# Four-layer convolution chain on one core: in the third layer, numerators made half a step ahead of their quotients, and a second of eighteen squares moved from GpSimd to VectorE

## The reference

```python
def _L2_conv_ref(x, A, Bc):          # DEG_P = 6, DEG_Q = 4, 3x3 windows
    xp = jnp.pad(x, ((0, 0), (0, 0), (pad, pad), (pad, pad)))
    wins = jnp.stack([xp[:, :, i:i + H, j:j + W] for i in range(K) for j in range(K)])
    pw = wins[..., None] ** jnp.arange(DEG_P, dtype=x.dtype)
    P = jnp.einsum('pbchwi,fcpi->fpbchw', pw, A)
    Q = 1.0 + jnp.abs(jnp.einsum('pbchwi,fcpi->fpbchw', pw[..., 1:1 + DEG_Q], Bc))
    out = jnp.sum(P / Q, axis=(1, 3))
    return jnp.transpose(out, (1, 0, 2, 3))
```

## Time and profile before

| | |
|---|---|
| time, median of 3 executions | 11572.25 us (11549.52 to 11573.89) |
| profiled execution: its own time | 11549.69 us |
| profiled execution: span of the trace | 11547.8 us |
| busy over the span | PE 8600.7, DVE 8534.8, ACT 6994.4, POOL 5920.0 us |
| third layer's pairs: first q block, last | 5994.0 us, 10554.8 us after the span's start |
| products of line 1360 in the whole run | 4232 to `l_r`, 528 to `l_rc` |

### The profile page before, as it was taken

How to read it: one execution, slowest core, us unless ns; L and a number is a source line. 1 busy time by engine, 2 the same in 40 slices (tenths; PEclk the granted TensorE clock), 3 DMA queues, 4 the chain that set the end, 5 groups by cost and what they waited for, 6 DMA issues and landing times. The chain is left out here.

```text
span 11547.8 us, 174635 instructions
## 1 busy us (share of the span) xinstructions
PE 8600.7 (74%) x48250; PEld 4203.0 (36%) x48250; DVE 8534.8 (74%) x10195; ACT 6994.4 (61%) x7795; POOL 5920.0 (51%) x2841
## 2 busy tenths in 40 slices
PE   0788758884888488853018888888888888885699
PEld 0566536663666366631002222222222222221233
DVE  1787668775777478754648888888888888886677
ACT  0455435553555255533438888888888888885454
POOL 0223223221333123210039999999999999995243
PEclk9899879987999689976559999999999999997899
DMA  2000000000000100011422232223322222224444
GB/s 90 1 0 0 15 23 0 0 11 26 0 0 7 30 1 0 0 38 56 148 83 59 67 65 60 59 59 66 65 61 59 59 63 65 64 59 100 122 115 99
DMA packets 254148, 548.42 MB, mean 47 GB/s; under 512 B 38656, under 2 KB 173088, under 8 KB 239552
## 3 DMA queue, kind: packets, MB, share of 16 engines
q1 hardware_dynamic: 253366, 539.26, 19.3%
HBM read 353.17 MB, written 185.94 MB: 47 GB/s over the span
## 5 line engine op out<-in xcount | busy, mean ns | idle before, releaser
L1232 POOL TENSOR_TENSOR l_a<-l_a 128x1018 f32<-128x1018 f32 x2248 | 4282.8, 1940 | 296.4 <-ACT l_a L1398 286.6
L1360 DVE TENSOR_TENSOR l_r<-l_pps,l_a 128x509 f32<-128x509 f32 x4232 | 2641.4, 679 | 641.3 <-PE l_pps L1245 641.3
L1398 ACT ACTIVATE l_a<-l_a 128x2036 f32<-128x2036 f32 x1193 | 2268.6, 1902 | 178.0 <-DVE l_a L1366 106.4
L1391 ACT ACTIVATE l_a<-l_qps 128x1018 f32<-128x1018 f32 x1725 | 1748.1, 1020 | 531.2 <-PE l_qps L1245 494.4
L1245 PE MATMUL l_qps<-l_mv,l_wst 123*128 123x509 bf16 x4246 | 1317.1, 393 | 865.8 <-DMA l_mv<-pw 577.0
L654 POOL TENSOR_TENSOR a_pr<-a_pr 128x768 f32<-128x768 f32 x384 | 898.7, 2340 | 1639.3 <-DVE a_pr L569 1624.2
L1245 PE MATMUL l_pps<-l_mv,l_wst 123*128 123x509 bf16 x4232 | 1356.6, 389 | 145.8 <-DVE l_r L1360 137.5
L454 POOL TENSOR_TENSOR a_pr<-a_qkv 128x768 f32<-128x768 f32 x128 | 386.7, 3040 | 2065.3 <-ACT a_qkv L696 2065.3
L683 ACT ACTIVATE a_g<-a_fps 128x512 f32<-128x512 f32 x1152 | 680.6, 597 | 989.8 <-PE a_fps L436 988.4
L436 PE MATMUL a_fps<-a_hbt,a_wfc 96*128 96x512 f32 x2304 | 1217.6, 664 | 70.3 <-ACT a_g L683 70.3
L407 PEld LDWEIGHTS a_cps<-a_wfp,a_g 128*128 128x128 f32 x9216 | 1120.7, 197 | 204.6 <-issue 154.8
(11 more groups left out here) (164 smaller groups left out, 11770.4 us busy)
## 6 DMA issues: line engine op xcount, KB each, us to landing
l_mv<-pw SPq DMA_DIRECT2D x1608, 79.5 KB
l_gx<-g SPq DMA_DIRECT2D x66, 1040.0 KB
planes<-l_s SPq DMA_DIRECT2D x67, 1018.0 KB, 4.6
l_sh<-planes SPq DMA_DIRECT2D x536, 127.2 KB, 6.3
pw<-pw_hi SPq DMA_DIRECT2D x165, 127.2 KB
pw<-pw_mid SPq DMA_DIRECT2D x165, 127.2 KB
pw<-pw_lo SPq DMA_DIRECT2D x165, 127.2 KB
a_tb<-g SPq DMA_DIRECT2D x16, 1031.9 KB
```

The lines of the kernel that those rows point to most:

```text
L1232: g.tensor_tensor(a, a, a, ALU.mult).then_inc(sq_p, 1)
L1360: v.tensor_tensor(to, pps[:, (2 * m + h) % P_BANKS, 0:SUB], pair_of(A, m)[:, h, :], ALU.mult).then_inc(mul_done, 1)
L1391: s_.activation(pair_of(A, s), q, ACT.Abs).then_inc(abs_a, 1)
L1398: s_.activation(a, a, ACT.Abs_reciprocal_sqrt, bias=1.0).then_inc(root_done, GROUP)
```

## The change

The numerator blocks are numbered b = 2m and 2m + 1 for pair m. Where PE made blocks 2m and 2m + 1 in step s = m + 8, it now makes blocks 2m + 1 and 2m + 2: the second block of this step's pair and the first block of the next one. And pair 14 of each eighteen joins pair 3 in the set that DVE squares, so POOL squares 16 of 18 instead of 17. Buffers, lags and every amount of matmul work stay the same.

```diff
 ABS_DVE = {1, 5, 8, 12, 15}
-SQ_DVE = {3}
+SQ_DVE = {3, 14}
...
                     last.then_inc(q_made, 1)
-                    m = s - LAG_P
-                    if m >= 0:
-                        sub, n = divmod(m, NPAIR2)
-                        for h in range(2):
-                            pe.wait_ge(mul_done, it * (2 * STEPS) + 2 * m + h - P_BANKS + 1 + 2 * A_PAIRS)
-                            product(0, sub, 2 * n + h, pps[:, (2 * m + h) % P_BANKS, 0:SUB]).then_inc(p_made, 1)
+                    for b in (2 * (s - LAG_P) + 1, 2 * (s - LAG_P) + 2):
+                        if b >= 0:
+                            sub, n = divmod(b, NBLK)
+                            pe.wait_ge(mul_done, it * (2 * STEPS) + b - P_BANKS + 1 + 2 * A_PAIRS)
+                            product(0, sub, n, pps[:, b % P_BANKS, 0:SUB]).then_inc(p_made, 1)
```

## The result

The changed kernel takes 11725.22 us in the median of 4 executions (11708.07 to 11751.85), the kernel before 11573.07 us beside it. The ratio is 1.0128 with a 95% interval of 1.0112 to 1.0144: slower by 1.3%. The direction was forecast, the size was not: 47 us were expected above the median of before, about 150 came, and 11,725 lies above the range.

A forecast was written before the change was run, and what follows sets the result against it. The ring PE -> DVE -> PE was taken to set the pace, not POOL. The order's -1.2 and the squares' +2.1 us a supertile gave +0.9, times 66 +59 us: 11,620 us forecast, range 11,465 to 11,700.

The forecast's parts named there:

- POOL is not the bound: Third layer: POOL only fills space between ACT and DVE; the rival that POOL is the bound had 11,453 us, chance 0.1.
- The five pairs that POOL was ahead: Counts by 8058.3 us: POOL's squares reach pair 1079, DVE's products 1074 pairs, so POOL is some five pairs ahead.
- The new squares: DVE's second square, two a supertile: 1.6 - 0.5 + 1.13 = 2.2, taken as +2.1 us; bounds 1.0 and 4.0.
- The 1.13: Price in us of the second-half square, right behind the output add, where POOL idles and nothing covers it.
- The 1.6: Price in us of the first-half square by the median; some 0.5 us of it falls into an existing DVE wait.
- The order: PE's new numerator order: feeds DVE one product sooner, holds PE around squares; net -1.2 us a supertile.
- the bound of -1.9: Best case for PE's numerator order, us a supertile: the walk through one supertile with nothing lost.
- bounded that at +0.2: Worst case for PE's numerator order, us a supertile: an earlier DVE only waits longer for POOL in its square.
- the forecast of +0.9: Whole third layer: -1.2 + 2.1 us a supertile, times 66 is +59 us; the slower outcome had chance 0.48.
- the gains of the walk, 0.6 and 1.4: Numerator order, us a supertile: output add after the gather 0.6 earlier; q blocks waiting for absolute values about 1.4.
- The second cost that I named: PE's last block of a step waits one product longer; q blocks and sums 0.6 us later around DVE's square.
- signs that I had named for my own outcome: DVE idle 9.7 to some 7 us, busy over 0.88; POOL about 0.88; 265 squares, mean above 1.5; longer PE waits.

The follow-up runs named there:

- the pair of runs with one reduction: DVE's square of pair 3 replaced by a one-input reduction, pair left unsquared: kernel before 11541.81 us; kernel with the new order alone 11396.65 us.
- the pair with two: DVE's squares of pairs 3 and 14 replaced by one-input reductions, pairs left unsquared: order of before 11581.65 us, changed kernel 11499.87 us.
- both squares late: Changed kernel with DVE's squares of pairs 3 and 14 moved behind the two products of their step: 11609.21 us, ratio 1.0022.
- the run with the late square: Kernel with the new order and only pair 3 squared on DVE; that square moved behind the two products of its step: 12071.4 us, ratio 1.0416.

## Why the prediction was right about the sign and wrong about the size

**POOL is not the bound: right.** Relieving it by the second square alone cost 1.3%, loading it with DVE's squares gave 1.2%. The five pairs that POOL was ahead said more than its busy share of 940. One reason why the share misleads is in the earlier trace rows too: a POOL square of 2.86 us counts as busy for 0.98 us in which DVE's holds it up. The Trainium skill's rule (Perfetto Trace Analysis, Identifying the Most-Contended Engine), by which the engine of highest occupancy is to be relieved first, would have sent one the wrong way here.

**The new squares: right in size, and in part by luck.** Forecast were 1.6 and 1.13 us from start to start, found 1.47 and 1.12 in the supertile shown. The 1.13 had a reason that held: POOL had run out of work there. The 1.6 was the median of pair 3's squares and held only because pair 14's falls near the end of a square of POOL in the changed kernel; with the order of before it takes 2.85, 2.76 from start to start. The second square alone cost 147 us, 2.2 us a supertile, where the sum had 2.1.

**The order: this step failed.** The sum had -1.2 us a supertile for it, and the run with the order alone shows +1.7 to +1.8. The mechanism that I wrote down was right: without contention the order gains 145 us, 2.2 us a supertile, more than I took and just past the bound of -1.9. But the price of the square that was already there was left as it was. I had written that an earlier DVE "only waits longer for POOL in its square", and bounded that at +0.2, as if the square would end at the same moment. POOL's squares stand 1.84 us apart. Before, DVE's mostly had 0.5 to 0.6 us of one left to wait for; in the changed kernel it drops near the start of one and waits 1.5 us. That is 2.46 x 2 - 1.47 - 1.62 = 1.8 us a supertile, or 121 us. To the forecast of +0.9 it adds 1.8, and what the order gains beyond my 1.2 goes off: 1.0 by the pair of runs with one reduction, nothing by the pair with two. That gives 1.7 to 2.7 us, and 2.25 were measured; a closer account is not shown. (The bound of -1.9 was also a slip: the gains of the walk, 0.6 and 1.4, add up to 2.0.)

**Banks.** The second cost that I named, PE held one product longer, agrees with the waits: PE's weight loads wait 896 us for DVE. That this hold costs time of its own is not shown: with reductions in the squares' place the new order gains in both kernels.

**The granted clock** was left out of the sum, and no run tests it by itself. It is 0.97 in the stretch of before and 0.95 after. Two supertiles of before, from one output add to the next:

```profile
7028.83:7095.84 67.01, 57.84 (x312) 16.49 (x312) 58.86 (x86) 60.36 (x50) 64.21 (x34) 1.00 0.28 63
7991.01:8059.52 68.51, 59.36 (x312) 16.72 (x312) 58.85 (x86) 60.77 (x50) 65.27 (x35) 0.98 0.29 62
```

DVE is busy for the same time in both. In the second one TensorE's clock stands at the lower of its two levels (1.2 instead of 2.4 GHz) for 3.4 us, from 8054.95 on, behind a wait of PE of 2.17 us, and the supertile takes 1.5 us more. Between 6900 and 10,400 us the lower level holds for 3.6 us a supertile before and for 6.5 after, against 2.2 with both squares late and 1.1 with the new order and one reduction. Seven supertiles of 49 before had none of it and take 67.0 to 67.2 us; five of 48 with the order alone had none and take 67.3. So the lower clock is probably part of the 2.25 us, and of what the contention costs; how large a part stays open.

**The sign** came out right by luck: it is the sum of a gain that was real and a loss that sat elsewhere than I had put it. The contention costs 2.0% in the changed kernel. Without it, with reductions in the squares' place, that kernel is 0.7% faster than before. Most signs that I had named for my own outcome came true as well: DVE busy at 0.89, POOL at 0.88, 265 squares on DVE with a mean of 1.95 us, longer waits of PE for products. (DVE's idle time ahead of products fell to 8.8 us a supertile, not to 7.) They fit any loss on DVE, and can't tell the mechanism that I had from the one that was there.

**How the two engines exclude each other.** The Trainium skill (SBUF — State Buffer, Who interferes with whom) has GpSimd and a VectorE instruction with two SBUF inputs exclude each other for a whole instruction, and whoever comes second is blocked until the first is through. The trace agrees in the squares of 1.5 to 2.8 us: each takes the rest of POOL's running square and 1.07 to 1.08 us, where one alone takes 1.21. The squares of 11.26 us do not follow it: DVE was waiting before five of POOL's squares had begun, and they all went ahead of it.

**What stays open.** What decides whether DVE's square gets the next turn or is passed over. In the run with the late square the 43 that were passed over had begun 0.90 to 0.96 us into a square of POOL, and eight at 1.32 to 1.34 were not passed over. In the run with the order alone 7 of 114 were, all of them 1.31 to 1.32 us in, and took 12.68 us. In the kernel before, four at 0.92 to 0.95 got the next turn. So the arrival does not decide it alone; what else does, I haven't tried.

## What to carry to other kernels

Where two engines exclude each other for whole instructions, the price of an instruction is not a constant that is read once from the trace: it is its own time plus the rest of the other's, and any edit that shifts its arrival reprices it, those that were there before too. Read the other engine's start next to each of its starts, and ask where the shifted one will land. And a busy share doesn't name the bound: count how far each stage is ahead of its consumer. Where PE waits longer, read its granted clock too.

## What the runs showed that was not expected

A DVE square with both inputs in SBUF can be kept out through six back-to-back squares of POOL, 11.26 us for an instruction of 1.21, and 12.68 us in 7 of 114 squares with the order alone. Moving one instruction by two others in DVE's list did this to 43 of 105 squares and cost 365 us of 11,707.
